# Criss-cross attention on one core: two channel tiles at a time, and the residual loaded into the accumulators

## What is computed

```
q = Wq x + bq    (64 channels)      k = Wk x + bk    (64 channels)      v = Wv x + bv    (512 channels)
eH[h,w,p] = q[:,h,w] . k[:,p,w]     (the pixel's column; p = h is masked out)
eW[h,w,p] = q[:,h,w] . k[:,h,p]     (the pixel's row)
attH, attW = softmax over the 192 scores of each pixel
out = gamma * (sum_p v[:,p,w] attH[h,w,p] + sum_p v[:,h,p] attW[h,w,p]) + x
```

## Time and profile before

| | us |
|---|---|
| three runs | 4829.86 (median), 4828.94, 4844.14 |
| profiled execution | 4835.99 |
| its span, first to last instruction | 4834.2 |
| PE busy | 3601.8 (75%) |
| DVE busy | 2321.5 (48%) |
| ACT busy | 1975.2 (41%) |
| POOL busy | 1220.7 (25%) |

### The profile page before, as it was taken

How to read it: one execution, slowest core, us unless ns; L and a number is a source line. 1 busy time by engine, 2 the same in 40 slices (tenths; PEclk the granted TensorE clock), 3 DMA queues, 4 the chain that set the end, 5 groups by cost and what they waited for, 6 DMA issues and landing times.

```text
span 4834.2 us, 92235 instructions
## 1 busy us (share of the span) xinstructions
PE 3601.8 (75%) x32472; PEld 2369.9 (49%) x32472; DVE 2321.5 (48%) x3322; ACT 1975.2 (41%) x3852; POOL 1220.7 (25%) x979
## 2 busy tenths in 40 slices
PE   4978778587885878858777587766887678874765
PEld 2435555355552555526554265543655445553655
DVE  6648443484334743357433564436543275433522
ACT  2425534154442544325443354333543245342632
POOL 0000342204321042311423014320143202431233
PEclk9989998798997989979898798987998889987656
DMA  7876699956998669986799867997599975999299
GB/s 281 288 226 218 180 280 292 276 188 192 296 282 272 189 186 301 294 257 197 198 291 288 249 195 213 299 274 253 167 252 299 260 254 160 268 305 239 76 263 270
DMA packets 995049, 1180.34 MB, mean 244 GB/s; under 512 B 48896, under 2 KB 788224, under 8 KB 988416
## 3 DMA queue, kind: packets, MB, share of 16 engines
q1 hardware_dynamic: 939264, 1023.06, 75.3%
q10 hardware_dynamic: 55296, 151.02, 8.5%
HBM read 834.15 MB, written 339.74 MB: 243 GB/s over the span
## 4 chain that ended last, share of the span: by engine, by line
issue 53%; PE 11%; DMA 10%; POOL 10%; SPq 9%; ACT 3%; DVE 2%; ACTq 0%; POOLq 0%; DVEq 0%
DMA xr<-x 6%; POOL e_grp L489 6%; SPq L387 5%; POOL xr L499 3%; DMA v_in<-v_pixel_major 3%; SPq L377 3%; PE banks L955 3%; PE banks L957 2%; PE banks L956 2%; POOL qk_lo L471 1%; SPq L323 1%; ACT acc L609 1%; PE banks L1027 1%; PE banks L1029 1%; PE banks L1028 1%
## 5 line engine op out<-in xcount | busy, mean ns | idle before, releaser
L955 PE MATMUL banks<-wv_hi,x_hi 128*128 128x512 f16 x2304 | 961.6, 417 | 401.0 <-DVE v_out L758 264.5
L758 DVE SCALAR_TENSOR_TENSOR v_out<-banks,proj,v_out 128x512 f16<-128x512 f32 x576 | 431.8, 750 | 1525.6 <-ACT v_out L560 1523.2
L499 POOL TENSOR_TENSOR xr<-xr,acc 128x768 f32<-128x768 f32 x384 | 721.7, 1888 | 1074.4 <-DVE acc L825 636.3
L956 PE MATMUL banks<-wv_lo,x_hi 128*128 128x512 f16 x2304 | 951.8, 413 | 0.0
L957 PE MATMUL banks<-wv_hi,x_lo 128*128 128x512 f16 x2304 | 945.3, 410 | 0.0
L609 ACT ACTIVATE acc<-banks,gbv_col,att 128x384 f32<-128x384 f32 x768 | 694.7, 996 | 302.7 <-POOL xr L499 183.3
L560 ACT ACTIVATE v_out<-banks,proj 128x512 f16<-128x512 f32 x576 | 390.6, 682 | 935.4 <-PE banks L957 757.6
L471 POOL TENSOR_TENSOR qk_lo<-qk_f,qk_hi 128x384 f16<-128x384 f32 x192 | 178.0, 927 | 2114.2 <-ACT qk_hi L568 2106.7
L1027 PE MATMUL banks<-prob_col,v_in 96*128 96x96 f16 x3072 | 479.1, 217 | 239.5 <-ACT acc L609 118.1
L1027 PE MATMUL banks<-prob_row,v_in 96*128 96x96 f16 x3072 | 472.1, 217 | 140.7 <-DVE acc L825 79.1
L955 PEld LDWEIGHTS banks<-wv_hi,x_hi 128*128 128x128 f16 x2304 | 244.0, 106 | 675.5 <-DVE v_out L758 276.7
(11 more groups left out here) (99 smaller groups left out, 6455.6 us busy)
## 6 DMA issues: line engine op xcount, KB each, us to landing
v_in<-v_pixel_major SPq DMA_DIRECT2D x768, 384.0 KB, 8.7
x_raw<-x SPq DMA_DIRECT2D x195, 768.0 KB, 6.5
v_pixel_major<-v_out SPq DMA_DIRECT2D x576, 256.0 KB, 4.7
x_next<-x SPq DMA_DIRECT2D x192, 768.0 KB, 6.1
xr<-x SPq DMA_DIRECT2D x384, 384.0 KB, 10.3
out<-xr ACTq DMA_DIRECT2D x384, 384.0 KB, 6.4
x_first<-x SPq DMA_DIRECT2D x24, 768.0 KB, 8.0
qk_halves<-qk_hi SPq DMA_DIRECT2D x192, 96.0 KB, 2.1
```

Of the source, the lines that this page charges most:

```text
L499: nc.gpsimd.tensor_tensor(xr[u][:, :], xr[u][:, :], acc[:, c * CPX:(c + 1) * CPX], ALU.add).then_inc(res_added, 1)
L758: nc.vector.scalar_tensor_tensor(out=v_out[tile % V_OUT][:, :, 1, :], in0=bank[tile % 2][:, :].rearrange("p (t c) -> p t c", t=CT), scalar ...
L955: nc.tensor.matmul(dst, s_hi, m_hi, start=(t == 0), stop=False)
L956: nc.tensor.matmul(dst, s_hi, m_lo, start=False, stop=False)
```

## The change

- **Blocks of 256 pixels.** 36 blocks of three items (two v tiles, then q and k with 256 columns), 108 items in all. `x_raw` rows become 1024 bytes per piece. `v_out` has three buffers, `qk_f32` one, and SP issues the store of a v tile one item later.
- **Two channel tiles at a time.** The group order becomes pair of tiles, column or row, strip group, tile. `v_in` holds 4 strips of two tiles (pieces of 1024 bytes, the same 384 KB per load, still 96 loads for an image). Transposes and splits of a strip group come with the first of its two groups. Normalisation happens in place in `prob`, four groups ahead; `e_grp` is gone.
- **Residual in accumulators.** There are two accumulators. For the first pair of tiles, x is loaded into them whole after the last score pair (4.7 MB, 2.4 MB, and 2.4 MB more at the sixth item of the statistics); for the second pair, each chunk is reloaded after its store has landed. All 192 groups are added by DVE (`add_group`); the column activation on ACT and the addition on POOL are gone. Before each store, ACT adds gamma * bv to the chunk in SBUF (48 activations of 128 x 768).
- **Stages.** Head 18 items with `load_qk` after the seventh (10 transfers: the low part of k is loaded once, and its matmul uses 64 partitions); the first six `v_in` loads are issued there too; 24 pairs with one item each; statistics 14 items; T with 21 items among the first 96 groups, 10 items with no group (the turn), 21 items among the last 96 groups. The scan has two buffers instead of four: ten pieces in the head, 14 in the pairs.

```diff
-    BLK = 4 * W
+    BLK = 256
+    TT = 2
+    TP = CT // TT
+    HALF = 2 * NG * TT
-    NXT = 4
+    NXT = 2
-    V_OUT = 4
+    V_OUT = 3
-    HEAD = 8
-    STATS = 5
+    QK_AT = 6
+    HEAD = 18
+    STATS = 14
+    TURN = 10
+    DEAL = (T_ITEMS - TURN) // 2
...
         def group_at(i):
-            return i // (2 * NG), (COL, ROW)[i // NG % 2], i % NG
+            return i // HALF, (COL, ROW)[i // (NG * TT) % 2], i // TT % NG, i % TT
...
+            def reload_residual(b, tt, c):
+                sp.wait_ge(out_stored[tt][c], b * (TP * 16) + 16 + 16)
+                px = slice(c * CH, (c + 1) * CH)
+                sp.dma_start(acc[tt][:, px], x_acc[b, TT + tt, :, px]).then_inc(acc_loaded[tt], 16)
...
+                wait_alone(sp, s_ready, (b + 1) * PAIRS)
+                sp.dma_start(acc[0][:, :], x_acc[b, 0, :, :]).then_inc(acc_loaded[0], 16)
+                sp.dma_start(acc[1][:, 0:HW // 2], x_acc[b, 1, :, 0:HW // 2]).then_inc(acc_loaded[1], 16)
                 for k in range(STATS):
                     if items:
                         item(b + 1, HEAD + PAIRS + k)
+                    if k == 5:
+                        wait_alone(sp, factor_row_ready, b + 1)
+                        if items:
+                            wait_alone(sp, xmax_own_ready, b + 3)
+                        sp.dma_start(acc[1][:, HW // 2:HW], x_acc[b, 1, :, HW // 2:HW]).then_inc(acc_loaded[1], 16)
...
-            def add_residual(b, i):
...
-                nc.gpsimd.tensor_tensor(
-                    xr[u][:, :], xr[u][:, :], acc[:, c * CPX:(c + 1) * CPX], ALU.add
-                ).then_inc(res_added, 1)
...
+            def store_chunk(b, g):
+                tp, o, h, tt = group_at(g)
+                px = slice(h // 2 * CH, (h // 2 + 1) * CH)
+                act.wait_ge(acc_added, b * GROUPS + g + 1 + ADDED0)
                 nc.scalar.activation(
-                    acc_strips[COL][:, h * G:(h + 1) * G, :], out_bank[g % OUTS], ACT.Identity,
-                    scale=att[:, O_FACTOR:O_FACTOR + 1], bias=gbv_col[:, t:t + 1],
-                ).then_inc(col_evac, 1)
+                    acc[tt][:, px], acc[tt][:, px], ACT.Identity, bias=gbv_col[:, tp * TT + tt:tp * TT + tt + 1]
+                ).then_inc(bias_added, 1)
+                act.wait_ge(bias_added, b * (CT * NCH) + tp * (TT * NCH) + (h // 2) * TT + tt + 1)
+                act.dma_start(out_acc[b, tp * TT + tt, :, px], acc[tt][:, px]).then_inc(out_stored[tt][h // 2], 16)
...
+            def add_group(b, g):
+                tp, o, h, tt = group_at(g)
+                if h == 0 and o == COL:
+                    done = FIRST_LOADS[tt] * 16 if tp == 0 else RESIDUALS[tt]
+                    wait_alone(dve, acc_loaded[tt], b * RESIDUALS[tt] + done)
...
+                a = acc_strips[tt][o][:, h * G:(h + 1) * G, :]
                 nc.vector.scalar_tensor_tensor(
                     out=a, in0=out_bank[g % OUTS], scalar=att[:, O_FACTOR:O_FACTOR + 1], in1=a,
                     op0=ALU.mult, op1=ALU.add,
-                ).then_inc(row_added, 1)
+                ).then_inc(acc_added, 1)
```

More of the change, by code:

```diff
@@ L364, in load_qk @@
                     sp.dma_start(k_hi[CQ:P, px], qk[b, 0, CQ:P, px]).then_inc(qk_loaded[c], 16)
[L365 to L376, removed]
+                    sp.dma_start(k_lo[:, px], qk[b, 1, CQ:P, px]).then_inc(qk_loaded[c], 16)
@@ L389, in batch @@
             def batch(b, items):
-                load_qk(b)
-                for k in range(HEAD + PAIRS):
+                for k in range(HEAD):
                     if items:
                         item(b + 1, k)
[L394 to L399, removed]
@@ L405, in batch @@
+                    if items:
+                        for c in scan_at_head(k):
+                            load_next((b + 2) % B, b + 1, c + NXT)
+                for p in range(PAIRS):
+                    if items:
+                        item(b + 1, HEAD + p)
+                    if items:
+                        for c in scan_at_pair(p):
+                            if c + NXT < SCAN:
+                                load_next((b + 2) % B, b + 1, c + NXT)
                 wait_alone(sp, s_ready, (b + 1) * PAIRS)
-                for i in range(XR):
-                    load_residual(b, i)
+                sp.dma_start(acc[0][:, :], x_acc[b, 0, :, :]).then_inc(acc_loaded[0], 16)
@@ L633, in batch @@
                         nc.scalar.activation(scaled[:, :, :], shift[:, :, :], ACT.Exp).then_inc(shift_exp, 1)
-                for i in range(AHEAD):
-                    high_parts(b, i)
+                    if items:
+                        item(b + 1, HEAD + PAIRS + k)
+                for j in range(AHEAD):
+                    high_parts(b, j)
+                SETTLE = 3
                 for k in range(T_ITEMS if items else GROUPS):
@@ L899, in batch @@
                         factor_row(b)
-                for i in range(AHEAD):
-                    low_parts(b, i)
+                        if items:
+                            see_all(b + 1)
+                    if items:
+                        item(b + 1, HEAD + PAIRS + k)
+                for j in range(AHEAD):
+                    low_parts(b, j)
                 for k in range(T_ITEMS if items else GROUPS):
@@ L1032, in batch @@
             def batch(b, items):
-                for k in range(HEAD + PAIRS):
+                for k in range(HEAD):
                     if items:
                         item(b + 1, k)
-                    if k >= HEAD:
-                        score_pair(b, k - HEAD)
+                for p in range(PAIRS):
+                    if items:
+                        item(b + 1, HEAD + p)
+                    score_pair(b, p)
                 for k in range(STATS):
```

406 lines of the change are left out of this document (206 added, 200 removed).

## The result

The changed kernel takes 5274.4 us (median of four runs, 5251.1 to 5292.5), the kernel before 4834.6 us on the same chip: ratio 1.0905, 95% interval 1.0855 to 1.0955, 9% slower. The forecast was 4735 us, in a range up to 4900.

What follows compares the result with a forecast made beforehand. Transfers were taken to bound the head and 240 us of T. Stages 88 + 121 + 41 + 318 plus 6 slack gave 574 us a turn; 4836.0 - 87 - 14 = 4735 us, range 4560 to 4900.

Steps and rivals of the forecast that it cites:

- Pairs: Score-pair stage of a turn: 121 us instead of 125.9, bounds 116 and 126; the 64-partition matmul has as many columns.
- Head: Opening stage of a turn, 18 items instead of 8: first pair at 88 us, before 65.0.
- rival B: Items stop behind long loads in SP's one queue, in head and statistics: 26 us a turn, 4917 us; chance 0.19.
- Statistics: Stage after the pairs, 14 items instead of 5: 41 us, before 18.2, bounds 33 and 57, set by transfers.
- What DVE takes over: Strided column addition in T taken at 1.0 us on DVE, which bounds the column halves: 73 and 60 us.
- A: Strides free on DVE: column addition 0.61 us, PE the bound of the column halves, 4591 us; chance 0.24.
- Rows, turn, tail: Rest of T, at 325 GB/s: row halves 86 and 64 us, item-only turn 29, tail 6 instead of 12.7.
- rival C: Transfers in T stay at 296 GB/s or reloads stall it: 10 to 18 us a turn, about 4830 us; chance 0.15.
- Last turn and prologue: Last turn 14 us less than 418, its T 276 instead of 290; prologue change 0, bounds -3 and +8.

Runs made afterwards that it cites:

- e1: The changed kernel with the low part of k loaded into all 128 partitions again and its score matmul on 128: 4746.2 us, ratio 0.9827.
- e5: e1 with column groups added at the contiguous positions of the rows (column result on wrong pixels): 4670.7 us, ratio 0.9649.
- e4: The changed kernel with both score matmuls on 64 partitions (q_lo x k_hi left out too): 4822.7 us in a single run.

## Why the prediction was wrong

**The step that failed** is *Pairs*: "The 64-partition matmul has as many columns. 121 us instead of 125.9; bounds 116 and 126." It counted columns, which are indeed the same, and set no price on following a 128-partition matmul by a 64-partition one. No row of before shows that sequence, so its cost was unknown and needed a bound of its own; mine bounded only the work on the blocks. Measured 182.9 us a turn. The 16 changes a pair and the lower clock behind them cost 62 us a turn beyond the forecast (67 against e1, whose pairs take 115.9), and 49 us in the last turn, whose pairs took 125 us instead of 76 (e1): some 480 us. e1, which differs in nothing but this, is 545 us faster: 70 a turn in seven turns, and 51 in the last. The Trainium skill, "TensorEngine Tiling (Array Packing)", section "Key Properties", says that changing the tiling mode drains TensorE. Read so that 64 partitions are another mode than 128, it agrees with the traces: each such change has a price, 0.125 or 0.235 us, and one from 128 to 96 none; that the price is a drain isn't shown. I had not weighed the sentence. It names no price; but 16 changes in each of 24 pairs are 384 a turn, at the prices measured 24 us of PE's time in the row pairs and 45 in the column pairs, and even an unpriced term repeated so often called for a rival on the slow side.

**Head** (88, measured 92.7; 97.4 in e1 with the two loads more): PE stands 27.8 us behind the burst (ACT waits 37.1 us for one v store) and begins again 54 us after the opening copy, as the forecast and rival B both had it. The items left then take 38.6 us, between the forecast's 34 and B's 43, so about half of B's ten microseconds in the head came. **Statistics** (41, measured 43.4): the forecast held and B didn't. B was to stop PE there for 23 us, and PE is busy 37.6 of the 43.4 us. B isn't the cause of the slower time: its 4917 us is 357 us under the result.

**What DVE takes over** (1.0 us): measured 0.97, so A's condition is false. DVE's busy time is 369 us in the third turn, forecast 380. The column halves took 74.1 and 58.0 us, forecast 73 and 60. But DVE is busy only 64 and 51 us of them, so it isn't the full bound that I made of it. A's price was wrong too: with the addition at 0.61 us e5 gained 75 us, not 144.

**Rows, turn, tail** (86, 64, 29, 6): measured 89.0, 64.0, 35.0, 5.8. The rates are 293 and 320 GB/s, not 325, and the turn is 6 us longer: part of rival C, 9 us of its 10 to 18. No transfer holds up the second pair's column half of the third turn; DVE waits for `acc` in the last turn alone, 39.9 us, where the forecast had 30.

**Last turn and prologue.** Without the failed step the forecast looks near: e1 has 4746 us. Part of that is luck. Its turns average 581.0 us, 7 more than forecast, 49 us in seven; its last turn takes 365.4 us and not 404. Of these 39 us, 13 are the head (first maximum 26.5 us after the copy, 39.4 before), which I had left as it was, and the rest is T, where I had 276 us and e1 has 250: the row halves reach 323 and 331 GB/s and end 20 us earlier than I had counted. The prologue's 0 held within 2 us.

## What to carry to other kernels

Before a matmul is narrowed to fewer partitions, look at what stands before and behind it on PE: rows saved brought nothing here (e4 with half the rows is slower than e1), and each change between 128 and 64 cost 0.12 to 0.24 us, so narrow ones belong in groups, or are filled up to 128 partitions, as e1 does. A cost that no row of the profile shows needs a bound from outside the pattern "same columns, same time". When a burst of loads fills the DMA engines, as here, make it wider (128 partitions) before moving it to another place or another queue.

## What the hardware showed that I had not expected

- A matmul of 96 columns on 64 partitions that follows one on 128, or the reverse, begins 0.17 instead of 0.045 us after it (strips along rows, full clock) and 0.40 instead of 0.165 (strips along columns, the 0.40 at either clock). Its weight load no longer overlaps the matmul before. From 128 to 96 partitions there is no such price.
- In the alternation of column strips PE has no idle time by its records, and yet the granted clock falls to 0.5; it averages 0.71 over the column pairs and 0.97 in e1.
- DVE's addition over a stride of 96 float32 costs 0.97 us for 384 columns, against 0.61 contiguous.
- Loads into 64 partitions: 223 GB/s at full share, from two queues 274; into 128 partitions 424.
